# Scores in fp32 by 32x32 array tiles instead of stacked bf16 parts, V in a ring, the loop written out

## The reference, cut to what matters

```python
h = layernorm(x)
q, k, v = h @ Wq + bq, h @ Wk + bk, h @ Wv + bv      # as 16 heads of 8
scores = q k^T / sqrt(8), where 0 <= i - j < 32, else -1e30
x = x + softmax(scores) v @ Wo + bo
h = layernorm(x)
u = gelu(h @ (W1 + scale * m1)^T + b1)               # 512 wide
out = x + u @ (W2 + scale * m2)^T + b2               # m1, m2: products of tokens 1 to 16
```

## Time and profile before

| | us |
|---|---|
| median of 3 runs (lowest to highest) | 155.63 (155.54 to 155.65) |
| the profiled execution | 154.6 |
| its span, first to last instruction | 152.8 |
| mean granted TensorE clock | 0.955 |

### The profile page before, as it was taken

How to read it: one execution, slowest core, us unless ns; L and a number is a source line. 1 busy time by engine, 2 the same in 40 slices (tenths; PEclk the granted TensorE clock), 3 DMA queues, 4 the chain that set the end, 5 groups by cost and what they waited for, 6 DMA issues and landing times.

```text
span 152.8 us, 5053 instructions
## 1 busy us (share of the span) xinstructions
PE 133.0 (87%) x1923; PEld 100.8 (66%) x1923; DVE 98.7 (65%) x281; ACT 89.4 (58%) x256; POOL 51.3 (34%) x78
## 2 busy tenths in 40 slices
PE   0657088689999999999999999897799999999992
PEld 0315067358788788788788787786566557777792
DVE  6687959563498598598598698957677455111021
ACT  3437327649778778778778678539721865152400
POOL 6278838970032033032032031405500069600000
PEclk9999857758999999999999999999999999999999
DMA  1694996987507738547928909720000000020222
GB/s 47 188 280 161 266 256 240 201 318 174 148 0 291 192 111 304 154 136 294 225 66 312 244 27 328 187 76 0 4 0 4 0 2 4 0 69 13 56 66 76
DMA packets 27312, 21.10 MB, mean 138 GB/s; under 512 B 1303, under 2 KB 23070, under 8 KB 27294
## 3 DMA queue, kind: packets, MB, share of 16 engines
q1 hardware_dynamic: 27294, 20.85, 45.6%
HBM read 10.88 MB, written 9.96 MB: 136 GB/s over the span
## 4 chain that ended last, share of the span: by engine, by line
PE 74%; ACT 12%; DVE 5%; issue 3%; SPq 2%; DMA 2%; POOL 1%; ACTq 0%; DVEq 0%
PE bank_s L458 17%; PE bank_o L490 11%; PE bank_s L469 9%; ACT V L628 6%; PE bank_qk L611 5%; PE bank_s L513 4%; PE bank_qk L422 4%; PE bank_v L611 4%; PE bank_o L513 3%; PE bank_v L428 3%; PE bank_qk L423 3%; PE bank_w L536 2%; PE bank_w L532 2%; ACT probs L684 2%; PE bank_t L416 2%
## 5 line engine op out<-in xcount | busy, mean ns | idle before, releaser
L458 PE MATMUL bank_s<-KS,QS 128*128 128x64 bf16 x512 | 35.9, 226 | 3.7 <-ACT probs L684 3.7
L458 PEld LDWEIGHTS bank_s<-KS,QS 128*128 128x128 bf16 x512 | 34.8, 165 | 6.4 <-ACT probs L684 5.7
L827 DVE TENSOR_REDUCE negmax<-bank_s 128x8 f32<-128x512 f32 x32 | 22.0, 689 | 19.9 <-PE bank_s L458 18.2
L684 ACT ACTIVATE probs<-bank_s 128x512 f32<-128x512 f32 x32 | 19.1, 597 | 19.1 <-PE bank_s L469 18.8
L490 PEld LDWEIGHTS bank_o<-V,probsT 128*32 128x32 f32 x1024 | 19.6, 114 | 14.7 <-issue 12.5
L628 ACT ACTIVATE V<-bank_v 32x64 f32<-32x64 f32 x128 | 27.3, 214 | 1.5
L490 PE MATMUL bank_o<-V,probsT 128*32 128x36 f32 x1024 | 23.3, 201 | 0.0
L840 DVE STREAM_TRANSPOSE probsT<-probs 128x512 f32<-128x512 f32 x32 | 22.5, 703 | 0.0
L285 POOL TENSOR_TENSOR q_parts<-rest,q_parts 128x256 bf16<-128x256 f32 x8 | 5.9, 742 | 47.2 <-ACT q_parts L628 47.2
L469 PE MATMUL bank_s<-negmax,ident_bf 128*128 128x512 bf16 x32 | 12.7, 395 | 0.5 <-DVE negmax_low L833 0.5
L469 PE MATMUL bank_s<-negmax_low,ident_bf 128*128 128x512 bf16 x32 | 12.6, 395 | 0.0
(11 more groups left out here) (109 smaller groups left out, 232.1 us busy)
## 6 DMA issues: line engine op xcount, KB each, us to landing
k_scr<-k_parts SPq DMA_DIRECT2D x8, 576.0 KB, 4.9
KS<-k_scr SPq DMA_DIRECT2D x8, 576.0 KB, 5.0
q_scr<-q_parts SPq DMA_DIRECT2D x8, 512.0 KB, 3.2
QS<-q_scr SPq DMA_DIRECT2D x32, 128.0 KB, 3.0
x_sb<-in_L_attn_x_dram SPq DMA_DIRECT2D x1, 768.0 KB, 5.5
out_dram<-y SPq DMA_DIRECT2D x3, 256.0 KB, 2.3
w<-in_L_ffn_W_dram SPq DMA_DIRECT2D x2, 256.0 KB, 5.5
x_sb<-in_L_attn_x_dram SPq DMA_DIRECT2D x2, 128.0 KB, 2.3
```

What stands on the lines that cost most here:

```text
L458: mm = nc.tensor.matmul(dst, QS[b][:, o, g].rearrange("p h t -> p (h t)")[:, j::BLOCKS], KS[b][:, o, g, j * WIN:(j + 2) * WIN], start=(i = ...
L684: nc.scalar.activation(probs[s % 2][:], bank_s[s % 2][:], ACT.Exp, scale=float(HD) ** -0.5).then_inc(probs_done, 1)
L827: nc.vector.tensor_reduce(negmax[s % 2][:], bank_s[s % 2][:].rearrange("p (a k) -> p a k", k=2 * WIN), AX.X, ALU.max, negate=True).then_in ...
```

## The change

It computes the scores from fp32 q and k. ScalarE adds the biases and writes q to `q_sb` and k to `k_all`, which keeps the keys of all chunks. wq and wk are permuted beforehand (three ScalarE copies at the start), so that in a group of 32 rows the four heads are interleaved. SyncE copies each head's rows of q (every fourth partition) into a place of its own in `Qm`, which is zero elsewhere: four DMAs a chunk from SBUF to SBUF, in place of ten through DRAM. A score tile of one block, head and group is one fp32 matmul on a 32x32 array tile (32 rows in, 32 queries out, 64 keys): 128 a chunk, alternating over four column tiles and two row tiles, in two halves of two groups (`scores(m)`). A bank now holds one group's eight blocks. The mask is laid into the bank before, by an identity matmul of 32x32 from `band` (which GpSimd builds for 32 rows and three DMAs copy to the others).

The centring moves from two matmuls on TensorE to one VectorE addition (`centre`) into a new tile `centred`, from which ScalarE takes the exponential. The matmuls of v are 32 small ones that write each head to its quadrant, and ScalarE spreads them with 4 copies a chunk; V is a ring of three chunks (24 blocks), without the copy of the last block. Values, normalising, turning, projecting and residual go by group and by chunk of 256 tokens, the values over four column tiles. Everything that split q and k, masks' slots, QS, KS and their memsets are gone. All loops are written out (`for k in range(NS + ...)`, 32 steps, one group of one chunk each). The second layernorm of tokens 0 to 511 goes from VectorE to GpSimd. There are four banks for scores, two for outputs, two for the rest.

```diff
@@ tiles and tensors
-        q_parts = two("q_parts", [P, SLOTS, CHUNK], BF16)
-        k_parts = two("k_parts", [P, SLOTS, KW], BF16)
-        QS = two("QS", [P, 2, NG, GH, CHUNK], BF16)
-        KS = two("KS", [P, 2, NG, KW], BF16)
-        V = two("V", [P, BLOCKS + 1, NG, VC])
+        q_sb = two("q_sb", [P, CHUNK])
+        Qm = two("Qm", [P, GH, CHUNK])
+        k_all = sb("k_all", [P, WIN + S])
+        V = sb("V", [P, RING * BLOCKS, NG, VC])
+        centred = two("centred", [P, BLOCKS * KW])
@@ SyncE
-            def restack(turn, b):
...
+            for c in range(NCH):
+                b = c % 2
+                if c < 2:
+                    sp.wait_ge(q_zero, c + 1)
+                sp.wait_ge(q_done, c + 1)
+                ge(sp, s_ps, 2 * (c - 1))
                 for hh in range(GH):
+                    sp.dma_start(Qm[b][hh::GH, hh], q_sb[b][hh::GH]).then_inc(q_in[b], 16)
@@ TensorE
+            def project_v(c):
+                pe.wait_ge(xT_done, c + 1)
+                cols = wv[:].rearrange("p (g h d) -> p h g d", g=NG, h=GH)
+                for j in range(BLOCKS):
+                    for hh in range(GH):
+                        mm = nc.tensor.matmul(bank_b[hh * WIN:(hh + 1) * WIN, CHUNK + j * WIN:CHUNK + (j + 1) * WIN],
+                                              xT[c % 2][:, j * WIN:(j + 1) * WIN], cols[:, hh],
+                                              start=True, stop=True, skip_group_check=True)
                 mm.then_inc(v_ps, 1)
-            def scores(turn, s):
...
+            def scores(m):
+                c, pair = m // 2, (2 * (m % 2), 2 * (m % 2) + 1)
+                b = c % 2
...
+                if m % 2 == 0:
+                    pe.wait_ge(q_in[b], 64 * (c // 2 + 1))
+                    pe.wait_ge(k_done, c + 1)
+                ge(pe, centred_done, 2 * (m - 1))
+                for hh in range(GH):
+                    for g in pair:
+                        rows, out_rows = slice(g * WIN, (g + 1) * WIN), slice(hh * WIN, (hh + 1) * WIN)
+                        one = ident_bf[rows, g * WIN:(g + 1) * WIN]
...
+                            nc.tensor.matmul(bank_s[g][out_rows].rearrange("p (j k) -> p j k", k=KW), one,
+                                             band[rows, 0:1].to_broadcast([WIN, BLOCKS, KW]),
+                                             start=True, stop=False, skip_group_check=True)
+                for j in range(BLOCKS):
+                    for hh in range(GH):
+                        for g in pair:
+                            rows, out_rows = slice(g * WIN, (g + 1) * WIN), slice(hh * WIN, (hh + 1) * WIN)
+                            k0 = c * CHUNK + j * WIN
+                            mm = nc.tensor.matmul(bank_s[g][out_rows, j * KW:(j + 1) * KW],
+                                                  Qm[b][rows, hh, j * WIN:(j + 1) * WIN], k_all[rows, k0:k0 + KW],
+                                                  start=False, stop=True, skip_group_check=True)
                 mm.then_inc(s_ps, 1)
-            def centre(turn, s):
...
+            def values(k):
+                c, g = k // NG, k % NG
...
+                if g == 0:
                     pe.wait_ge(v_done, c + 1)
+                    ge(pe, x1_done, c - 1)
                 pe.wait_ge(probsT_done, k + 1)
+                for t in range(TILES):
                     for w in range(2):
+                        for q in range(QB):
+                            j = QB * t + q
+                            key = (BLOCKS * c + j - 1 + w) % (RING * BLOCKS)
+                            mm = nc.tensor.matmul(bank_o[c % 2][q * WIN:(q + 1) * WIN,
+                                                                (t * NG + g) * VC:(t * NG + g + 1) * VC],
+                                                  probsT[k % 2][:, j, w], V[:, key, g],
+                                                  start=(w == 0), stop=(w == 1), skip_group_check=True)
                 mm.then_inc(pv_ps, 1)
+            for k in range(NS + 5):
+                c, g = k // NG, k % NG
+                if g == 0 and c + 1 < NCH:
+                    project(c + 1)
+                if g == 1 and c + 1 < NCH:
+                    project_v(c + 1)
+                if g == 3 and c + 2 < NCH:
+                    turn_x(c + 2)
+                if k % 2 == 0 and k // 2 + 1 < 2 * NCH:
+                    scores(k // 2 + 1)
+                if g == 0 and k >= NG + 1:
+                    out_proj(c - 2)
+                if 2 <= k < NS + 2:
+                    values(k - 2)
+                if g == 3 and k >= NG:
+                    turn_att(c - 1)
...
@@ ScalarE
+            def copy_qk(c):
...
+            def spread_v(c):
+                act.wait_ge(v_ps, c + 1)
+                ge(act, pv_ps, NG * (c - 1))
+                if c < RING:
+                    act.wait_ge(v_one, GH)
+                blocks = slice(BLOCKS * (c % RING), BLOCKS * (c % RING + 1))
+                for hh in range(GH):
+                    rows = slice(hh * WIN, (hh + 1) * WIN)
+                    cp = ident_act(V[rows, blocks, :, hh * HD:(hh + 1) * HD],
+                                   bank_b[rows, CHUNK:].rearrange("p (j g d) -> p j g d", j=BLOCKS, g=NG))
+                cp.then_inc(v_done, 1)
+            for k in range(NS + 2):
+                c, g = k // NG, k % NG
+                if g == 0 and c + 1 < NCH:
+                    copy_qk(c + 1)
+                if g == 0 and k >= NG + 1:
+                    copy_attT(c - 2)
+                if g == 3 and c + 2 < NCH:
+                    copy_xT(c + 2)
+                if k < NS:
+                    softmax_exp(k)
...
@@ VectorE
+            def row_max(k):
+                dve.wait_ge(s_ps, k // 2 + 1)
+                nc.vector.tensor_reduce(negmax[k % 2][:], by_block(bank_s[k % NG][:]), AX.X, ALU.max,
+                                        negate=True).then_inc(max_done, 1)
+            def centre(k):
+                dve.wait_ge(max_done, k + 1)
+                ge(dve, probs_done, k - 1)
+                nc.vector.tensor_tensor(by_block(centred[k % 2][:]), by_block(bank_s[k % NG][:]),
+                                        negmax[k % 2][:].unsqueeze(2).to_broadcast([P, BLOCKS, KW]),
+                                        ALU.add).then_inc(centred_done, 1)
+            def turn_probs(k):
                 dve.wait_ge(probs_done, k + 1)
                 ge(dve, pv_ps, k - 1)
+                nc.vector.transpose(probsT[k % 2][:].rearrange("p j w q -> p (j w q)"), probs[k % 2][:]).then_inc(probsT_done, 1)
+            for k in range(NS + 6):
+                c, g = k // NG, k % NG
+                if k < NS:
+                    row_max(k)
+                if g == 2 and 1 <= c <= NCH:
+                    denominators(c - 1)
+                if k < NS:
+                    centre(k)
+                if 1 <= k < NS + 1:
+                    turn_probs(k - 1)
+                if g == 2 and 1 <= c <= NCH:
+                    normalise(c - 1)
+                if g == 0 and 2 <= c:
+                    residual(c - 2)
+                if g == 1 and 2 <= c:
+                    ln2_stats(c - 2)
+                if k == 0:
+                    dve.wait_ge(rstd1_done, 3)
+                    ln1_norm(2)
+                    ln1_var(4 * TILES, NT)
...
```

More of the change, by code:

```diff
@@ L23 @@
 BF16 = mybir.dt.bfloat16
-U32 = mybir.dt.uint32
 AX = mybir.AxisListType
@@ L357, in _ @@
             add_bo(0, 2 * TILES)
+            ln1_norm(4)
             add_bo(2 * TILES, 4 * TILES)
+            ln1_norm(5)
             add_bo(4 * TILES, NT)
[L360 to L367 removed]
+            ln1_norm(6)
+            ln1_norm(7)
             def ln2_rstd(f):
@@ L464, in centre @@
-            def centre(turn, s):
-                k = SU * turn + s
-                pe.wait_ge(max_parts, k + 1)
-                for part, last in ((high_half(negmax[s % 2]), False), (negmax_low[s % 2][:], True)):
-                    mm = nc.tensor.matmul(bank_s[s % 2][:].rearrange("p (a k) -> p a k", k=2 * WIN), ident_bf[:],
-                                          part.unsqueeze(2).to_broadcast([P, UB * NG, 2 * WIN]),
-                                          start=False, stop=last, skip_group_check=True)
-                mm.then_inc(centred_ps, 1)
@@ new lines, in values, with turn_att, out_proj @@
+                mm.then_inc(pv_ps, 1)
+            def turn_att(c):
+                pe.wait_ge(att_done, c + 1)
+                for t in range(TILES):
+                    mm = nc.tensor.transpose(bank_o[c % 2][:, t * P:(t + 1) * P], att[:, t], ident[:])
+                mm.then_inc(attT_ps, 1)
+            def out_proj(c):
+                pe.wait_ge(attT_done, c + 1)
+                for t in range(TILES):
+                    mm = nc.tensor.matmul(bank_o[c % 2][:, CHUNK + t * P:CHUNK + (t + 1) * P],
+                                          attT[:, t * P:(t + 1) * P], wo[:], start=True, stop=True)
+                mm.then_inc(wo_ps, 1)
@@ L595, in _ @@
```

(19 more changed lines are left out.)

752 lines of the change are left out of this document (232 added, 520 removed).

## The result

The changed kernel takes **172.88 us** (170.41 to 173.80) against 155.64 of the kernel before: ratio **1.102 [1.090, 1.115]**, slower by a tenth, where 139.2 was forecast and 131 to 162 was the range. The profiled execution took 173.8 us for a span of 172.0. Executions of one kernel differ here by up to 5%; the ratios compare the faster ones, while the traces of after, e2, e6, e7, e8, e9, e10 and e11 are of slower ones, so chunk lengths of two kernels compare to about 2 to 3% only.

A forecast was written before the change was run, and what follows sets the result against it. TensorE was taken to bound the kernel before; afterwards TensorE (10.0) and VectorE (9.6) nearly level, 10.2 us a chunk. Start 30 + loop 68.9 + tail 37.5 + 1.8 + 1.0 = 139.2 us, range 131 to 162.

The forecast's parts named there:

- TensorE in a chunk after the change: Loop: TensorE's work per 256-token chunk, kept work plus new score, mask and v matmuls, summed to 10.0 us.
- four rivals: Values' rate 146 us (0.2); tiles not parallel 175 (0.14); lower clock 151 or 160 (0.12); VectorE alone 135 (within forecast's 0.5).
- anything else: Whole kernel: outcomes outside forecast and rivals, chance 0.04, of it 0.01 faster and 0.03 no change.
- Rival 2: Loop: tiles run no more than two side by side, score matmul 56 ns, chunk 15.4 us, 175 us; chance 0.14.
- Score matmul: Loop, TensorE: one 32x32-tile score matmul priced at 28 ns, four side by side (14 to 56); 3.6 us a chunk.
- VectorE, 9.6 us a chunk: Loop: maximum, centring, turn at 2.0 us a step, plus normalising, residual, statistics; VectorE forecast busy over 85%.
- q path: Loop: projection, ScalarE bias and four DMAs take 5 to 6 us in series, priced at 0 to 1 us a chunk.
- the q DMA ends last ahead of the scores: Loop: one of the signs listed in advance that would show the forecast wrong.
- rival 3: Loop: clock falls to half when TensorE waits; chunk 12 us, 151 us, or 13.3 and 160; chance 0.12.
- Start: Ahead of the loop: first maximum at 17.5 us against 24.94, maximum 2 at 25, maximum 4 at 30.
- Tail: Behind maximum 31: first up matmul at +3.6 us, mostly TensorE feed-forward work, 37.5 us in all, nothing gained.

The follow-up runs named there:

- e2: Changed kernel plus 16 one-column matmuls ahead of each half chunk's scores, 512 TensorE instructions more doing next to no work: 179.88 us, ratio 1.161.
- e6: Changed kernel without the DMAs for q; ScalarE writes q to each head's place with a column of ones and zeros as scale: 168.83 us, ratio 1.088.
- e7: e6 and e1 together in the changed kernel, 7076 TensorE instructions: 164.87 us, ratio 1.056.
- e8: e6 plus one score matmul for four heads, its 128 stationary columns contiguous, 4748 TensorE instructions: 158.70 us (151.78 to 158.75).
- e9: Changed kernel with x's large load ahead of the mask's three copies and V's zeros and ones ahead of the third rstd: 169.57 us, ratio 1.093.
- e10: e8 reordered: attT's copy ahead of q's, residual one step later, x's turn and q/k projection one step earlier: 147.67 us, ratio 0.941.
- e11: e10 with e9's start: 143.52 us (138.65 to 145.17) beside 154.59 of the kernel before.
- e12: Changed kernel with e10's three moves, keeping its 8036 TensorE instructions: 169.47 us, ratio 1.094.
- e1: Changed kernel with v by two large matmuls a chunk for 32 small, 16 ScalarE copies for 4, 7076 TensorE instructions: 164.19 us, ratio 1.061.
- e5: Score matmuls alone on constant data: 1280 written out, four passes of a hardware loop over 256, then 256 written out: 135.67 us (one run).
- e3: Changed kernel with one score matmul for four heads, q's columns read at a 32-byte stride, 4748 TensorE instructions: 178.75 us, ratio 1.154.

## Why the prediction was wrong

The step that failed is "TensorE in a chunk after the change". It summed what the instructions take to run, 10.0 us, and had no term for what they take to arrive: 3.7 packets of code at 3.9 us, 14.5 us a chunk, with 14.87 measured.

| kernel | TensorE instructions a chunk | packets | x median distance | chunk measured |
|---|---|---|---|---|
| after | 952 | 3.72 | 3.89: 14.5 | 14.87 |
| e12 | 952 | 3.72 | 3.77: 14.0 | 14.16 |
| e9 | 952 | 3.72 | 3.81: 14.2 | 14.61 |
| e6 | 952 | 3.72 | 3.78: 14.1 | 14.33 |
| e2 | 1016 | 3.97 | 4.02: 16.0 | 15.83 |
| e1, e7 | 832 | 3.25 | 3.95, 3.89: 12.8, 12.6 | 13.45, 13.50 |
| e8, e10 | 544 | 2.13 | not reached | 11.93, 10.22 |

The count of after is 256 score, 128 value, 64 v, 16 mask and 12 other matmuls a chunk, each with a weight load; a matmul in fp32 counts as two. The distance is the median over the whole trace. In any kernel, packets a chunk times their mean distance give the chunk, so the last columns agree by themselves; what the table shows is that the distance stays near 3.9 us while the count changes, and cannot be brought down. In none of the fourteen kernels run do two packets start less than 3.3 us apart. Kernels that ask for them faster sit at a median of 3.8 to 4.0, at either level of the clock: those of after that lie wholly in recorded full clock are 3.54, 3.66 and 3.87 us apart (leaving out one of the tail), the 15 in recorded half clock have a median of 3.86. The kernel before had about half the instructions and 12 packets at a median of 8.2 us, and TensorE has no gap over 0.3 us put down to "issue" in its trace. None of the four rivals was this, and the 0.04 left for anything else held nothing for slower. Rival 2's 175 us lies near the result by chance only: its price of a score matmul did not come true. (The range ended at 162 all the same, though rival 2 had a chance of 0.14.) The number that could have warned me was on the page, 12 packets of code, beside a change that doubles the instructions; that a packet takes 3.9 us it did not show.

The Trainium skill (Runtime: NRT & Kernel Launch, "Instruction fetch mechanics") states blocks of 16 KiB, 256 instructions, and a cost of crossing one that is mostly hidden. The packet's size agrees with the runs, and the gaps every 256 instructions too. "Mostly hidden" agrees with e8 and does not with e5, where every block that is new costs 1.4 to 2.0 us of standing from the 449th instruction on, nor with after, where 13 blocks cost 1.0 to 2.2 us each.

The steps of the prediction one by one:

- **Score matmul, 28 ns (14 to 56)**: right. The timeline of after has 128 instructions, 64 matmuls, at full clock in the row below: 23 ns each; at the lower clock, most of the loop, 32 (2.04 us). Rival 2 (56 ns) is out. The Trainium skill's floor of 25 ns between starts (TensorE: Matmul & The Clock Gate, "Wait — 56ns, not 53.3ns?"), weighed in the prediction, disagrees with these 11 ns an instruction as it did with the earlier trace rows.

```profile
27.91 1.45 PE L354 MATMUL bank_s<-k_all,Qm 32*32 32x64 f32 x128
```

- **VectorE, 9.6 us a chunk** (its terms add up to 9.5): right in its parts (maximum 671 ns, centring 678, turn 704) and never the bound: busy 60% of the loop (56.88 of 95.55 us, the window below), where over 85% was forecast.
- **q path, 5 to 6 us in series, 0 to 1 us a chunk**: underpriced, and "the q DMA ends last ahead of the scores" came true. Issues took 2.9 us in the chain above and the landing 3.8, 7.3 us from the projection's end. Its net cost is small only because code was awaited anyway: 2 us in all by e6.
- **Clock (rival 3)**: its condition came true, its price was hidden. The granted clock in the loop is 0.5 in most slices, far past 35 us, and 0.61 in the mean of the window from maximum 4 to shortly before the end of the loop, below. There TensorE is busy 76.66 of 95.55 us: 11.9 us a chunk, where 10.0 was forecast, and 2.9 idle. So without any limit of supply the lower clock alone could have taken the chunk to about 12 (an estimate from this window). That it does not set the 14.87 rests on e2, on e5's gaps and on the packets' distances at either level. In e1, e7 and e8 it may cost more (e8's scores take 3.52 us for 1.89 at the lower level); that was not separated, nor whether the standing for code is what made it fall.

```profile
32.34:127.89 95.55, 76.66 (x3080) 60.01 (x3076) 56.88 (x116) 33.61 (x75) 17.02 (x18) 0.61 0.05 13
```

- **Start**: maximum 0 at 17.87 (17.5 forecast), the third at 24.82 (25), maximum 4 at 32.34 (30), behind q 1 (2.32 us of standing from 25.36) and the first wait for code (1.50 us at 29.74).
- **Tail**: 39.0 (37.5). From the first up matmul to the end it is 33.8, the sum's own 33.9; the first up comes 5.2 us behind maximum 31 (3.6), after the weight update at half clock (2.07 and 1.71 us).

## What to carry to other kernels

Count an engine's instructions as a resource of its own: on TensorE 256 written-out instructions needed 3.8 to 4.0 us here, so a stage whose instructions, weight loads counted, take less than 15 ns each on average is bound by its code (3.9 us / 256), whatever runs side by side in the array. Make fewer, wider matmuls (e8: a quarter of the score instructions for the same scores), or keep dense stretches in a hardware loop (e5 shows it for score matmuls alone; it was not tried in the whole kernel). A wait that is taken away shows its worth only where the wait below it is gone too: the same three moves took the chunk from 11.93 to 10.22 us in e10, and gained 1.3 us in all, no more than the noise, in e12. And read a clock of 1.00 ahead of a trace's first recorded change with care: compare the pace of one kind of instruction with a stretch whose level is recorded.

## What the runs showed of the hardware

- Written-out TensorE code came in packets of 16384 bytes, 256 instructions, never closer than 3.3 us (all fourteen kernels) and at a median of 3.8 to 4.0 us where it was asked for faster. A hardware loop of four such blocks ran its second to fourth pass without a gap (e5).
- A stationary operand of 128 fp32 columns read at a stride of 32 bytes took 120 ns an instruction at either level of the clock (e3, 3.9 us for 32), a contiguous one 59 at full clock and 110 at the lower (e8, 1.89 and 3.52 us; 54 by the chain).
- 32x32 tiles over eight places of the array ran one fp32 instruction of 64 columns each 11 ns at full clock (1.45 us for 128) and each 16 ns at the lower (2.04 us; 2.03 in e5).
- The page gives the clock as 1.00 ahead of the first recorded change. In e8 and e10, where that is at 47.94 and 47.58 us, 32 score instructions took 3.5 us before it and 1.9 behind it.
